# Second attention, last thirteen steps: the first batch's second turn, its logits and its counts one to two steps later

## The reference

```python
x = x + attn_a(layernorm(x))   # 16 heads, relative position bias
x = x + ffn(layernorm(x))      # top-1 routing over 8 experts
x = x + attn_b(layernorm(x))   # 16 heads of 8, with a geometric gate
x = x + ffn(layernorm(x))      # the same routed experts again
```

## Time and profile before

| | |
|---|---|
| median of 3 runs | 1083.83 us |
| lowest, highest | 1083.58, 1083.98 us |
| profiled execution, its own time | 1086.94 us |
| its span, first to last instruction | 1084.8 us |
| mean granted TensorE clock | 0.934 |
| TensorE, VectorE, ScalarE, GpSimd busy | 89%, 72%, 55%, 31% |
| second attention's last steps (86 on) | 984 to 1011.5 us |
| second batch's projection | 1011.5 to 1018.8 us |
| second batch's routing, then the experts | from 1018.8, from 1044 us |

### The profile page before, as it was taken

How to read it: one execution, slowest core, us unless ns; L and a number is a source line. 1 busy time by engine, 2 the same in 40 slices (tenths; PEclk the granted TensorE clock), 3 DMA queues, 4 the chain that set the end, 5 groups by cost and what they waited for, 6 DMA issues and landing times. The chain is left out here.

```text
span 1084.8 us, 18594 instructions
## 1 busy us (share of the span) xinstructions
PE 962.4 (89%) x6220; PEld 626.3 (58%) x6220; DVE 776.0 (72%) x2343; ACT 593.6 (55%) x1171; POOL 333.3 (31%) x418
## 2 busy tenths in 40 slices
PE   6899999999999999999955687789999999999647
PEld 4767667666666677677644564344444444444437
DVE  6667658677577777677663589888888888886525
ACT  3767658667576666666621256243556555657312
POOL 2431213121122111112133504724534454332435
PEclk9899999999999999999956888888999999999669
DMA  6520000000000000000072200000000000000351
GB/s 189 122 57 2 1 1 1 1 1 1 2 1 1 1 1 1 2 2 1 2 236 65 65 3 1 1 0 1 1 2 1 1 2 1 1 2 1 117 179 34
DMA packets 43306, 29.91 MB, mean 28 GB/s; under 512 B 9264, under 2 KB 39909, under 8 KB 43213
## 3 DMA queue, kind: packets, MB, share of 16 engines
q1 hardware_dynamic: 41164, 24.63, 8.1%
q0 software_dynamic: 2048, 4.11, 1.2%
HBM read 20.34 MB, written 10.64 MB: 29 GB/s over the span
## 5 line engine op out<-in xcount | busy, mean ns | idle before, releaser
L632 ACT ACTIVATE attn_a_prob<-attn_a_score,attn_a_m_all 128x128 f32<-128x128 f32 (+7 forms) x256 | 188.9, 741 | 52.2 <-DVE attn_a_m_all L552 48.3
L1123 ACT ACTIVATE attn_b_probT<-attn_b_st 128x1024 f32<-128x1024 f32 (+1 forms) x192 | 145.2, 808 | 128.6 <-PE attn_b_st L905 127.0
L548 DVE TENSOR_REDUCE attn_a_m_far<-attn_a_score 128x1 f32<-128x512 f32 (+3 forms) x192 | 105.6, 550 | 79.6 <-PE attn_a_score L460 77.4
L472 PE MATMUL attn_a_slot<-tab,attn_a_prob 128*128 128x128 f32 x1152 | 149.6, 274 | 1.4 <-ACT attn_a_prob L632 1.2
L472 PEld LDWEIGHTS attn_a_slot<-tab,attn_a_prob 128*128 128x128 f32 x1152 | 132.4, 141 | 9.8 <-issue 2.1
L484 PE MATMUL attn_a_o<-attn_a_ptsa,Vd 128*64 128x512 f32 x288 | 137.4, 606 | 0.0
L484 PE MATMUL attn_a_o<-attn_a_ptsb,Vd 128*64 128x512 f32 x288 | 137.4, 606 | 0.0
L970 DVE CUSTOM_DVE_ANT_0 attn_b_slot<-attn_b_slot,later 128x128 f32<-128x128 f32 (+3 forms) x256 | 118.6, 521 | 18.3 <-PE attn_b_slot L880 18.2
L641 ACT ACTIVATE attn_a_ptsa<-attn_a_slot 128x512 f32<-128x512 f32 x144 | 85.9, 596 | 81.8 <-PE attn_a_slot L472 81.1
L880 PE MATMUL attn_b_slot<-KS,attn_b_alone 128*128 128x512 f32 (+2 forms) x384 | 123.1, 412 | 4.6 <-POOL attn_b_alone L1154 2.5
L552 DVE CUSTOM_DVE_ANT_0 attn_a_score<-attn_a_score,bias_near,attn_a_m_far 128x256 f32<-128x256 f32 (+2 forms) x192 | 107.4, 560 | 6.9 <-DVE attn_a_m_far L548 0.2
(11 more groups left out here) (288 smaller groups left out, 1846.3 us busy)
## 6 DMA issues: line engine op xcount, KB each, us to landing
moe_weights_w<-in_L_ffn_w_dram SPq DMA_DIRECT2D x32, 256.0 KB, 4.4
to_experts<-xn SPq DMA_DIRECT2D x2, 1056.0 KB, 13.0
moe_experts_xe<-to_experts SPq DMA_DIRECT2D x16, 132.0 KB, 2.6
bias_by_query_and_key<-bias_by_distance SPq DMA_DIRECT2D x2, 1024.0 KB
bias_near<-bias_by_query_and_key SPq DMA_DIRECT2D x2, 1024.0 KB, 6.8
rows<-in_L_attn_a_x_dram SPq DMA_DIRECT2D x2, 512.0 KB, 5.2
moe_weights_b<-in_L_ffn_b_dram SPq DMA_DIRECT2D x16, 64.0 KB, 5.0
moved<-rows SPq DMA_DIRECT2D x2, 512.0 KB
```

The lines of the kernel that those rows point to most:

```text
L472: ins = nc.tensor.transpose(dst[:, jj * P:(jj + 1) * P], probs(g)[:, 2 * jj + half, i * P:(i + 1) * P], ident[:, :])
L548: nc.vector.tensor_reduce(least, score[t % 2][:, at:at + nk - win], AX.X, ALU.min).then_inc(far_done, 1)
L632: nc.scalar.activation(probs(g)[:, j, 0:nk], score[t % 2][:, at:at + nk], ACT.Exp, bias=m_all[:, j:j + 1], scale=-1.0, accum_out=rowsum[g ...
L1123: nc.scalar.activation(probT[n % 2][:, two, lo:], st[:, two, lo:], ACT.Exp, scale=-1.0).then_inc(exp_done, 1)
```

## The change

One table is changed. The second turn of the first batch (`xt`, 1) is done in step 93 instead of 92, the logits of chunk 0 in step 94 instead of 92, the counts of chunk 0 and the logits of chunk 1 in step 95 instead of 93, the counts of chunk 1 in step 96 instead of 94. The computation is the same.

```diff
     END = STEPS - LAG
     BESIDE = {END: (("ot", 0),), END + 1: (("y", 0), ("ot", 1)), END + 2: (("y", 1),), END + 5: (("xt", 0),),
-              END + 6: (("xt", 1), ("logit", 0)), END + 7: (("count", 0), ("logit", 1)), END + 8: (("count", 1),)}
+              END + 7: (("xt", 1),), END + 8: (("logit", 0),), END + 9: (("count", 0), ("logit", 1)), END + 10: (("count", 1),)}
```

## The result

The changed kernel took 1086.51 us in the median of 13 runs (1083.87 to 1088.37), the kernel before 1083.74 (1082.78 to 1086.80) in the runs beside it: a ratio of 1.0025, 95% interval 1.0016 to 1.0034. It is slower, where no change was forecast, and 1086.51 lies above the range. Later comparisons made the size smaller. With 24 more runs of the changed kernel (1.0010 [0.9997, 1.0023] and 1.0016 [1.0004, 1.0027]) the mean of its 37 runs is 1085.89, against 1084.33 for 199 runs of the kernel before: **+1.56 us**, standard error 0.26, or 0.14%. Single executions spread far: 1081.45 to 1087.89 before, 1081.65 to 1088.37 after. The shift runs through all of them: the tenth, fiftieth and ninetieth percentile lie 1.9, 1.4 and 1.6 us later.

A forecast was written before the change was run, and what follows sets the result against it. It took a TensorE-ScalarE loop and two chains meeting at the attention's end as the bound; about 1 us gained earlier was lost waiting for the last counts, sum 0.0, forecast 1083.8 us, range 1082.5 to 1085.0.

The forecast's parts named there:

- rival (d): End of the stage: routing on VectorE 0.3 to 0.9 us later, as the clock falls already in step 95; 1084.4 us, chance 0.14.
- The other sign of being wrong: Sign against the forecast: TensorE's granted clock from 1009 to 1016 us differs from that of the kernel before.
- Counts 1: Chunk 1's counts, moved to step 96, hold up the last turn; reciprocal at 1010.62 against 1010.63, whole gain lost.
- Counts 0 and logits 1: Steps 93 to 95: choice takes 1.22 us, placing 1.45; step 95's value products start at 1007.31, 1.0 us earlier than before.
- the ends of -0.2 and +0.5: Range in us around the predicted difference of 0.0 at the stage's end, for unknown delays of exponentials and second placing.
- From there to the end: After the stage's reciprocal: nothing is changed and the projection follows the reciprocal, so no further difference.
- Sum: 0.0 us: Whole kernel: predicted net difference of the change, giving 1083.8 us on the median's scale.
- rival (c): Experts: a later start prolongs the low clock, +1.7 us, up to +2.2 with late routing (1086.0 us); chance 0.08.
- chain B: End of the second attention: logits, choice and placing of two chunks on VectorE; before, through 2.70 us ahead of the reciprocal.

The follow-up runs named there:

- the masks after the choice and the extra matmuls: Changed kernel with GpSimd's step-95 masks waiting for the first choice, plus thirteen matmuls with unused results: 1082.59 us, ratio 0.9986 to the kernel before.
- the first form of extra matmuls: Kernel before plus five matmuls with unused results ahead of the experts' first matmul, waiting until 12 of 16 scatters landed: 1087.67 us, ratio 1.0027.
- a stall of 0.2 us: Kernel before plus one small VectorE copy after the attention's last VectorE instruction: +1.0 us, ratio 1.0005.

## Why the prediction was wrong

**What held.** The replay of the chains was right to about 0.1 us up to the first choice. From step 92's exponentials the others started at 2.49, 4.73 and 6.88 us (foretold 2.55, 4.81, 6.86), the first choice at 6.44 (6.31). TensorE idles 1.42 us ahead of the last counts, released by VectorE's marks (foretold 1.5); ScalarE's copy lies 1.56 us ahead of the turn's start and so is over 0.96 before it (foretold about 1); the reciprocal has no idle time before it, where it was 2.70. The last turn was at the low level (1.09 us), and the clock fell ahead of it 10.4 us after step 92's exponentials in both kernels. So it did not fall already in step 95, as rival (d) had it for its own few tenths. Other executions show that this can happen: with the masks after the choice and the extra matmuls it fell at 8.31 and the stage took 12.11 instead of 11.90, and in the kernel before with the first form of extra matmuls it fell at 7.44 and the stage took 12.47 instead of 11.93. The other sign of being wrong, another clock from 1009 to 1016, is there if the microseconds are taken as they stand: the rise in the projection is at 1014.32 instead of 1015.88. That is the 1.60 us by which the whole execution ran earlier, and the low stretch is 6.82 us long in both. The hole in front of the counts has moved to the end of the stage and taken the whole gain, as "Counts 1" said.

**The term that was mis-sized** is in "Counts 0 and logits 1": "A choice takes 1.22 us". It took 1.74. The move had put the first choice beside the masks of step 95. I had written that GpSimd's queue keeps its order, which is so, and did not ask what now runs at the same time. In the trace of before the same masks were at 1007.51 and VectorE's L1087 beside them at 1007.60 took 0.33 us, against 0.16 at 1009.30 in the changed kernel; that row was in front of me, and I put the longer placing (1.70 us instead of 1.45) down to how it meets the counts. Even the comparison was uneven: 1.45 runs to the start of the next choice, and the first placing's own end is at 1.53. The first placing then started at 8.18 instead of 7.81 and the reciprocal at 12.29 instead of 11.93. This 0.36 lies inside the ends of -0.2 and +0.5 that I gave, but for another reason than the one I gave.

**The step that failed** is the one that puts all behind the stage at nothing: "From there to the end nothing is changed", with "Sum: 0.0 us". 36 us after the stage, those tenths cross the edge of the clock's rise, and the experts take 39.58 us instead of 38.02: +1.56 us. This is the mechanism of rival (c), and its price of 1.7 was nearly right. Its condition, chain B "more than about 0.3 us later than I say", was met as it stands, with 0.36, though a stall of 0.2 us suffices too. Its chance of 0.08 was too low: the sum itself could be 0.5 late by the ends that I gave. A cliff beside the path should have been weighed with the whole spread of the stage's own estimate.

**The spread.** My own range used 0.4 us, from three runs. That was chance: single executions of the kernel before cover 6.4 us. A range for the median of a dozen runs, with standard errors near 0.4, needed about 1 us more at each end from that alone. The three runs had also put the level too low, 1083.83 against 1084.33 in the mean of all. So of the 2.7 us between forecast and measurement 0.5 are that level, 1.56 the change, and 0.6 the chance of the first thirteen runs of the changed kernel, whose median of 1086.51 stands against a mean of 1085.89 over all 37. Without that chance the changed kernel would still lie above the range.

**What stays open.** Why so many executions come to the experts at nearly the same distance from the clock's last fall. If it were random, a shift of 0.35 us could cost only a small part of 1.56 in the mean. The profiles suggest that it is settled ahead of the changed steps: in 17 of the 20 the fall ahead of the last turn comes 10.2 to 10.5 us after step 92's exponentials, whatever the order behind them, and in the other three at 7.44, 8.31 and 11.59. What settles it there, and in how many executions it comes out otherwise, no run took apart. And with one to three profiles for each kernel, what share of a kernel's executions lies on which side of the edge is not known; the 1.8 us that the profiles give and the 1.56 of the mean leave room for some on the other side.

## What to carry to other kernels

Work moved along a queue must be compared with what every other engine does in that new moment, GpSimd against VectorE above all: here GpSimd's own queue did not change, and yet a 0.19 us instruction of VectorE took 0.44. Where TensorE comes out of a long idle time into a long stage, look in the trace for where the clock rises after the start; an earlier change of 0.2 us cost 1.5 there by the profiles (1.0 in the mean of the times), and what a change is worth can be measured cleanly only once the stage starts at the high level. Extra matmuls did that here when they left a hole of only 0.70 us and were over before the work arrived; with a hole of 3.06 us they gained nothing, and placed too late they cost 1 and 3 us. And take the spread of single executions from more than three runs.

## What the runs showed of the hardware

**VectorE beside GpSimd.** L1069 and L1070, each with two inputs in SBUF and 32 elements per partition, took 0.44 us when GpSimd's masks (0.77 us for two) had begun 0.01 us before them, and 0.19 and 0.18 when the masks were kept away. The Trainium skill, page "SBUF — State Buffer", section "🔬 SBUF: two separate sides", says that the two engines share a port pair as an exclusive lock: whichever starts first has it for its whole instruction and the other fully blocks, for a VectorE instruction with two SBUF inputs against a GpSimd one that reads SBUF. By that rule the masks should hold up just these two, and the trace agrees; by it alone, the second would not start before the lock is free, and how a profile shows a blocked instruction (here as a longer one) no run takes apart.

**The clock's rise has an edge.** In the eleven profiles without extra matmuls the high level came back 30.72 us behind the last fall where the experts' first matmul stood up to 27.48 us behind that fall, and 34.12 to 34.14 us behind it where the first matmul stood at 27.68 or later. The same 16 matmuls take 3.5 to 3.7 us when the clock is high from the start, 4.6 to 4.7 just short of the edge (5.2 where the start was a microsecond earlier) and 5.9 to 6.3 beyond it.
